# A vision tower's last LayerNorm without its mean, and uneven expert slices

## The reference

```
y       = layernorm(h)                                # no gain, eps 1e-5
logits  = y @ gate_w.T ; top 6 of 64 experts ; scores = softmax(top 6)
lattice = sum over chosen e of scores[e] * (y @ lattice_weights[e])
proj    = lattice @ out_w.T + out_b
f       = y + proj
out     = h + (f - mean(f)) * rsqrt(var(f) + 1e-5) * ln_g + ln_b
```

## Time and profile before

| | us |
|---|---|
| timed runs | 1074.19, 1078.10, 1079.18; median 1078.1 |
| profiled execution, own time | 1073.91 |
| its span, first to last instruction | 1072.0 |
| TensorE busy | 962.2 (90%) |
| VectorE busy | 617.9 (58%) |
| ScalarE busy | 397.2 (37%) |
| GpSimd busy | 151.3 (14%) |
| mean granted TensorE clock | 0.981 |

### The profile page before, as it was taken

How to read it: one execution, slowest core, us unless ns; L and a number is a source line. 1 busy time by engine, 2 the same in 40 slices (tenths; PEclk the granted TensorE clock), 3 DMA queues, 4 the chain that set the end, 5 groups by cost and what they waited for, 6 DMA issues and landing times.

```text
span 1072.0 us, 36541 instructions
## 1 busy us (share of the span) xinstructions
PE 962.2 (90%) x17004; PEld 619.3 (58%) x17004; DVE 617.9 (58%) x773; ACT 397.2 (37%) x522; POOL 151.3 (14%) x158
## 2 busy tenths in 40 slices
PE   4899999999989998999899899999888899688885
PEld 3567667667656633676567667657215677533342
DVE  2268458727844221577268458733153677779887
ACT  2442333233223486232332233233775676321100
POOL 6000000000000000000000000020010765234421
PEclk9999999999999999999999999999999899679998
DMA  6220130022021301310220230020001000000000
GB/s 197 94 79 3 60 93 24 4 94 79 4 79 61 114 6 37 109 33 4 94 79 3 67 91 18 3 94 18 14 16 42 2 2 1 2 1 1 1 11 11
DMA packets 25918, 46.78 MB, mean 44 GB/s; under 512 B 9949, under 2 KB 11000, under 8 KB 25125
## 3 DMA queue, kind: packets, MB, share of 16 engines
q1 hardware_dynamic: 24118, 42.47, 12.8%
q0 software_dynamic: 1456, 1.63, 0.6%
q10 hardware_dynamic: 192, 0.33, 0.1%
HBM read 30.25 MB, written 10.89 MB: 38 GB/s over the span
## 4 chain that ended last, share of the span: by engine, by line
PE 70%; DVE 13%; issue 6%; ACT 4%; POOL 2%; DMA 2%; SPq 1%; POOLq 0%; DVEq 0%
PE PSALL L1309 22%; PE PSALL L1277 8%; PE PSALL L1168 5%; PE PSALL L1300 5%; PE PSALL L1252 4%; PE PSALL L1182 4%; PE PSALL L536 3%; DVE WORK L1523 3%; PE PSALL L437 3%; DVE WORK L1013 2%; PE PSALL L523 2%; PE PSALL L1367 2%; DVE WORK L1542 2%; PE PSALL L1145 2%; PE PSALL L1296 2%
## 5 line engine op out<-in xcount | busy, mean ns | idle before, releaser
L1542 DVE STREAM_TRANSPOSE WORK<-PSALL 128x1024 f32<-128x1024 f32 x128 | 152.4, 1229 | 251.2 <-PE PSALL L1277 251.2
L1309 PEld LDWEIGHTS PSALL<-EW,WORK 128*64 128x64 f32 x4096 | 221.8, 138 | 72.7 <-issue 48.3
L1309 PE MATMUL PSALL<-EW,WORK 128*64 128x128 f32 x4096 | 247.6, 276 | 14.0 <-DVE WORK L1542 13.7
L1442 ACT ACTIVATE X<-PSALL,TABLES 128x1024 f32<-128x1024 f32 x128 | 141.8, 1114 | 306.5 <-PE PSALL L1309 306.5
L1523 DVE STREAM_TRANSPOSE WORK<-PSALL 128x1024 f32<-128x1024 f32 x84 | 104.3, 1241 | 32.8 <-PE PSALL L1168 31.0
L334 POOL DMA_DIRECT2D WORK<-MIXED x32 | 17.6, 550 | 665.5 <-ACT MIXED L1433 555.1
L1424 ACT COPY SPEC<-PSALL 128x400 f32<-128x400 f32 x64 | 54.4, 850 | 138.6 <-PE PSALL L1182 132.9
L1182 PEld LDWEIGHTS PSALL<-TABLES,WORK 128*64 128x64 f32 x2000 | 67.5, 139 | 47.3 <-DVE WORK L1523 31.4
L1013 DVE TENSOR_TENSOR WORK<-PSALL,X 128x832 f32<-128x832 f32 x80 | 79.3, 1017 | 16.8 <-PE PSALL L523 15.3
L1182 PE MATMUL PSALL<-TABLES,WORK 128*64 128x64 f32 x2000 | 81.1, 228 | 7.5 <-DVE WORK L1523 3.8
L1476 ACT ACTIVATE WORK<-PSALL,B 128x1024 f32<-128x1024 f32 x64 | 68.2, 1113 | 8.3 <-PE PSALL L1367 7.4
(11 more groups left out here) (157 smaller groups left out, 1153.5 us busy)
## 6 DMA issues: line engine op xcount, KB each, us to landing
SW<-in_spec_w SPq DMA_DIRECT2D x160, 80.0 KB, 2.7
spec_scr<-MIXED SPq DMA_DIRECT2D x24, 400.0 KB, 3.2
SPEC<-spec_scr SPq DMA_DIRECT2D x32, 200.0 KB
WORK<-spec_scr SPq DMA_DIRECT2D x16, 200.0 KB
WORK<-in_coords_w SPq DMA_DIRECT2D x2, 1024.0 KB, 4.8
XC<-in_coords_c SPq DMA_DIRECT2D x2, 1024.0 KB, 7.3
WORK<-MIXED SPq DMA_DIRECT2D x40, 40.0 KB
WORK<-MIXED POOLq DMA_DIRECT2D x32, 40.0 KB
```

What stands on the lines that cost most here:

```text
L1309: m = pe.matmul(PS[2 * p + z][64 * j:64 * j + 64, 2 * b * GRID:(2 * b + 2) * GRID], G[:, n % 2, b, h:h + 2, :, t].rearrange("p q o -> p (q ...
L1442: nc.scalar.activation(X[:, n].rearrange("p b (z d) c w -> p d z b (c w)", z=2)[:, p, :, :, 2 * t * GRID:2 * (t + 1) * GRID], PSALL[:, 2 * ...
L1542: nc.vector.transpose(G[:, n % 2, 2 * x + y].rearrange("p h o v -> p o h v"), PSALL[:, 4 + 2 * x:6 + 2 * x, :].rearrange("p k (h o v) -> p ...
```

## The change

The columns of out_w (laid out as 128 x 64, twice) and out_b are centred over the 64 features by the VectorE before step m = 2 of the last head; F then has a mean of zero by itself. `centre_last` is gone; GpSimd squares F directly. The slices end at images 7, 14, 21, 28 and 32. The last LayerNorm has five parts, of 8, 8, 8, 4 and 4 images; the first four lie in the loop, each with its variance and, one step later (SCALE_AT), its reciprocal and scale. Projection 6 moves from behind the loop to n = 142. For the last part the ScalarE squares (Square) while the VectorE multiplies by ln_g.

```diff
-ZT = NT // NZ
+ZI = [0, 7, 14, 21, 28, NIMG]
+ZT = 7 * TOK
-OUTPUT_AT = [84, 104, 136]
-PROJECT_AT = [n + 2 * i for n in OUTPUT_AT for i in range(LB // BC)]
+LASTS = [slice(0, 8), slice(8, 16), slice(16, 24), slice(24, 28), slice(28, NIMG)]
+PROJECT_AT = [84, 86, 104, 106, 136, 138, 142]
 ADD_AT = [n + 2 for n in PROJECT_AT]
-CENTRE_AT = [n + 6 for n in OUTPUT_AT]
-FINISH_AT = [n + 12 for n in OUTPUT_AT]
+VARIANCE_AT = [96, 116, 146, 152]
+SCALE_AT = [n + 2 for n in VARIANCE_AT]
...
@@ tail_tensor, broadcast
-                    pe.wait_ge(lo_ready, -(-(z + 1) * ZT // CT))
+                    pe.wait_ge(lo_ready, slice_chunks(z))
...
@@ tail_scalar, behind the loop over the slices
-            deviation(2, LK - 1)
+            act.wait_ge(f_ready, NC)
+            nc.scalar.activation(SQ[:, LASTS[-1]], F[:, LASTS[-1]], ACT.Square).then_inc(last_squared, 1)
+            deviation(2, len(LASTS) - 1)
...
@@ tail_pool, square; finished(k) is the gain and the residual of part k
+                    pool.wait_ge(f_ready, a.stop // BC)
+                    nc.gpsimd.tensor_tensor(SQ[:, a], F[:, a], F[:, a], ALU.mult).then_inc(squared, 1)
...
+            for k in range(len(LASTS) - 1):
                 square(2, k)
+                if k < 2:
+                    finished(k)
+            finished(2)
+            finished(3)
...
@@ tail_vector, in_head
+                if m == 2:
+                    dve.wait_ge(tail_w, 16 * TAIL_LOADS)
+                    link(nc.vector.reduce_sum(mw[:], WO[:], AX.X))
+                    link(nc.vector.reduce_sum(mo[:], OB[:], AX.X))
+                    link(nc.vector.tensor_scalar(mw[:], mw[:], 1.0 / GRID, None, ALU.mult))
+                    link(nc.vector.tensor_scalar(mo[:], mo[:], 1.0 / GRID, None, ALU.mult))
+                    nc.vector.tensor_tensor(WO[:], WO[:], mw[:].broadcast_to([128, GRID]), ALU.subtract).then_inc(ow_centred, 1)
+                    nc.vector.tensor_tensor(OB[:], OB[:], mo[:].broadcast_to([TOK, GRID]), ALU.subtract).then_inc(ob_centred, 1)
...
@@ tail_vector, in the loop
-                    if n in CENTRE_AT:
-                        centre_last(CENTRE_AT.index(n))
-                    if n in FINISH_AT:
-                        finish_last(FINISH_AT.index(n))
+                    if n in VARIANCE_AT:
+                        last_variance(VARIANCE_AT.index(n))
+                    if n in SCALE_AT:
+                        last_scale(SCALE_AT.index(n), F, ln_ready)
...
@@ tail_vector, behind the loop
-                centre_last(LK - 1)
-                finish_last(LK - 1)
-                a = slice(NIMG - LB, NIMG)
-                dve.wait_ge(ln_ready, LK)
-                link(nc.vector.tensor_tensor(TMP[:, a], TMP[:, a], rows(LNG[:], LB), ALU.mult))
+                k = len(LASTS) - 1
+                a, n = LASTS[k], NIMG - LASTS[k].start
+                dve.wait_ge(f_ready, NC)
+                nc.vector.tensor_tensor(TMP[:, a], F[:, a], rows(LNG[:], n), ALU.mult).then_inc(last_gained, 1)
+                last_variance(k)
+                dve.wait_ge(last_gained, 1)
+                last_scale(k, TMP, ln_ready)
+                dve.wait_ge(ln_ready, k + 1)
                 nc.vector.tensor_tensor(TMP[:, a], TMP[:, a], H[:, a], ALU.add).then_inc(last_ready, 1)
```

More of the change, by code:

```diff
@@ L113, in rows_step, with slice_tokens, slice_chunks @@
     return 6 + (i - ROWS_AT - 22) // 2 if i in (ROWS_AT + 22, ROWS_AT + 24) else None
+def slice_tokens(z):
+    return slice(ZI[z] * TOK, ZI[z + 1] * TOK)
+def slice_chunks(z):
+    return -(-ZI[z + 1] // BC)
 SELECTED = EXPERTS // 16
@@ L341, in tail_sync @@
             sp.dma_start(WE, w_expert).then_inc(we_in, 16)
-            for k in range(LK):
-                a = slice(k * LB, (k + 1) * LB)
-                if k < LK - 1:
+            for k, a in enumerate(LASTS):
+                if k < len(LASTS) - 1:
                     sp.wait_ge(out_ready, k + 1)
@@ L534, in expert_products @@
                     pe.wait_ge(lt_ready, z - 1)
+                w = slice_tokens(z).stop - slice_tokens(z).start
                 for i in range(2):
-                    m = pe.matmul(PS[4 + z % 2][64 * i:64 * i + GRID, 0:ZT], WE[:, ep + i, :], ZX[:, (n + i) % ZR, :],
+                    m = pe.matmul(PS[4 + z % 2][64 * i:64 * i + GRID, 0:w], WE[:, ep + i, :], ZX[:, (n + i) % ZR, 0:w],
                                   start=(ep == 0), stop=(ep == PAIRS - 2), tile_position=(0, 64 * i), skip_group_check=True)
@@ L540, in output_projection @@
             def output_projection(c):
-                pe.wait_ge(lt_ready, -(-(c + 1) * CT // ZT))
+                pe.wait_ge(lt_ready, [z for z in range(NZ) if ZI[z + 1] >= (c + 1) * BC][0] + 1)
+                pe.wait_ge(ow_centred, 1)
                 if c == 0:
@@ L578, in deviation @@
             def deviation(n, k):
-                a = slice(k * LB, (k + 1) * LB)
+                a = slice(k * LB, (k + 1) * LB) if n < 2 else LASTS[k]
                 act.wait_ge(var_ready, n * LK + k + 1)
@@ L680, in tail_scalar @@
                     deviation(2, z - 2)
+                if z == NZ - 1:
+                    deviation(2, z - 1)
                 act.wait_ge(zx_used, (z + 1) * PAIRS // 2)
-                nc.scalar.copy(LT[:, z * ZT:(z + 1) * ZT], PS[4 + z % 2][:, 0:ZT]).then_inc(lt_ready, 1)
-            deviation(2, LK - 1)
+                t = slice_tokens(z)
+                nc.scalar.copy(LT[:, t], PS[4 + z % 2][:, 0:t.stop - t.start]).then_inc(lt_ready, 1)
+            act.wait_ge(f_ready, NC)
+            nc.scalar.activation(SQ[:, LASTS[-1]], F[:, LASTS[-1]], ACT.Square).then_inc(last_squared, 1)
+            deviation(2, len(LASTS) - 1)
         def outside_sums_out(act, c):
@@ L708, in square @@
             def square(n, k):
-                a = slice(k * LB, (k + 1) * LB)
-                pool.wait_ge(centred, n * LK + k + 1)
-                nc.gpsimd.tensor_tensor(Y[:, a, 1, :] if n < 2 else SQ[:, a], TMP[:, a], TMP[:, a], ALU.mult).then_inc(squared, 1)
+                if n < 2:
+                    a = slice(k * LB, (k + 1) * LB)
+                    pool.wait_ge(centred, n * LK + k + 1)
+                    nc.gpsimd.tensor_tensor(Y[:, a, 1, :], TMP[:, a], TMP[:, a], ALU.mult).then_inc(squared, 1)
+                else:
+                    a = LASTS[k]
+                    pool.wait_ge(f_ready, a.stop // BC)
+                    nc.gpsimd.tensor_tensor(SQ[:, a], F[:, a], F[:, a], ALU.mult).then_inc(squared, 1)
             pool.wait_ge(mix_full.sem, PASSES * LAYERS * mix_full.stride)
@@ L807, in tail_pool, with finished @@
             pool.wait_ge(hl_ready, LK)
-            for k in range(LK):
-                square(2, k)
[L810 to L816, removed]
+            def finished(k):
+                a = LASTS[k]
+                n = a.stop - a.start
+                pool.wait_ge(ln_ready, k + 1)
+                nc.gpsimd.tensor_tensor(TMP[:, a], TMP[:, a], LNG[:].unsqueeze(1).broadcast_to([TOK, n, GRID]), ALU.mult
+                                        ).then_inc(scaled, 1)
+                pool.wait_ge(scaled, k + 1)
+                nc.gpsimd.tensor_tensor(TMP[:, a], TMP[:, a], H[:, a], ALU.add).then_inc(out_ready, 1)
+            for k in range(len(LASTS) - 1):
+                square(2, k)
+                if k < 2:
+                    finished(k)
+            finished(2)
+            finished(3)
         def tail_vector(dve):
@@ L997, in add_projection, with last_variance, last_scale @@
                                             F[:, a, :], ALU.add).then_inc(f_ready, 1)
[L999 to L1006, removed]
+                def last_variance(k):
+                    a = LASTS[k]
+                    if k < LK:
+                        dve.wait_ge(squared, 2 * LK + k + 1)
+                    else:
+                        dve.wait_ge(last_squared, 1)
+                    link(nc.vector.reduce_sum(st[:, 1, a], SQ[:, a], AX.X))
+                    nc.vector.tensor_scalar(st[:, 1, a], st[:, 1, a], 1.0 / GRID, EPS, ALU.mult, ALU.add).then_inc(var_ready, 1)
+                def last_scale(k, src, done):
+                    a = LASTS[k]
+                    dve.wait_ge(dev_ready, 2 * LK + k + 1)
+                    link(nc.vector.reciprocal(st[:, 3, a], st[:, 2, a]))
+                    nc.vector.tensor_tensor(TMP[:, a], src[:, a], over(st[:, 3, a], a.stop - a.start), ALU.mult).then_inc(done, 1)
                 for n in range(0, NZ * PAIRS, 2):
@@ L1012, in tail @@
                         dve.wait_ge(zx_used, (n - ZR) // 2 + 1)
-                    nc.vector.tensor_tensor(ZX[:, n % ZR:n % ZR + 2, :], PSALL[:, n % 4:n % 4 + 2, 0:ZT],
-                                            YT[:, z * ZT:(z + 1) * ZT].unsqueeze(1).broadcast_to([128, 2, ZT]), ALU.mult
+                    t = slice_tokens(z)
+                    w = t.stop - t.start
+                    nc.vector.tensor_tensor(ZX[:, n % ZR:n % ZR + 2, 0:w], PSALL[:, n % 4:n % 4 + 2, 0:w],
```

(1 more changed line is left out.)

12 lines of the change are left out of this document (9 added, 3 removed).

## The result

The changed kernel takes 1065.54 us (median of 5 runs, 1062.67 to 1069.06) against 1078.1 (1074.19 to 1079.18); the ratio is 0.9906, 95% interval 0.9884 to 0.9928. The profiled execution took 1065.44 us, its span 1063.6, against 1073.91 and 1072.0. The forecast was -9.0 us for such an execution; measured are -8.5. The ratio is the one on record; the quotient of the two medians is 0.9883, 12.6 us, and holds more of the scatter that is told of next.

What follows compares the result with a forecast made beforehand. TensorE and VectorE take turns, TensorE slightly slower per step and stalled by VectorE's LayerNorm work. Terms +3.4 - 7.4 - 4.7 - 0.3 = -9.0 us: 1069.1 us against the median 1078.1, range 1063.5 to 1074.3.

Steps and rivals of the forecast that it cites:

- the first two terms: Wider slices up to the first queued projection, +3.4 us; expert loop from there to the last product, -7.4 us.
- The wide slices: Expert loop before the first projection: 42 steps at 455 instead of 416 columns cost +3.4 us, at most 4.1.
- the sixth chunk: Slice 2 needs the sixth of eight score chunks, not the fifth; no wait counted, 1.1 us at most.
- The stalls: TensorE standing still in the later expert loop: 1.0 us per 8-image part, 2.9 in the narrow slice.
- The rule weighed: VectorE op with two SBUF inputs contends with GpSimd; scale of images 24 to 27 might lose up to 1.27 us.
- The tail: From the end of the last product to the last addition: 4.84 us instead of 9.56, so -4.7.
- The store: Last store after the last op, with half the bytes: -0.3 us, between 0 and -1.3.
- Centring the weights: Six small VectorE ops before m = 2 of the last head: cost 0, or 1.3 us without idle cover.
- (B): Narrow slice: weight loads, 1.0 us in a row, bound the 0.66 us step; -6.5 us, 1071.6 us; chance 0.07.
- (C): Tail: Square needs another table than the square root, two loads of 1.28 us; -8.2, 1069.9 us; chance 0.05.
- (D): Expert loop: TensorE's granted clock falls to half; +25 us, 1094 us, slower than before; chance 0.03.
- Rival A: Loop gains only -3.3 us, narrow slice crowded with VectorE work, wide steps cost +4.1; -4.2, 1073.9 us; chance 0.17.

## Why the prediction was right

- *The number.* 1069.1 us was given for the median, 1065.54 came. By the stretches with the end of the span the change is -9.3 against -9.0; the rest of the 12.6 us between the medians lies outside them, and the median of 1078.1 that the forecast started from was the highest of the three of the kernel before.
- *Who paces the loop* was right: TensorE's steps plus its stalls. Its account gave 45.9 us for the second stretch after, and 45.91 were measured (in the account 41.0 should be 40.9, which changes nothing); the half for before, 53.3, was 0.7 too long against 52.6, most of the difference between -7.4 and -6.7. That 45.9 was hit to the hundredth is luck: 1.0 us of it is a hold-up that the walk did not hold, and without it the stretch is 44.95. So is the sum of the first two terms: the first was 0.8 too high and the second 0.7 too low, and they cancel.
- *The wide slices*, +3.4 forecast, +2.6 measured. The step of a pair was right on both engines. The term was mis-sized because I charged every pair. Some time up to pair 41 is not set by pairs: behind each of three chains of choice the TensorE waited 0.55 us for GpSimd's scores (L702 before, L722 now), and now 0.36 to 0.37. These waits shrink, 0.5 us in all; I had not counted that. The other 0.3 us is not traced to its steps. That a broadcast would wait for the sixth chunk did not happen. The first of the three waits, before and after:

```profile
958.15 0.66 PE L487 MATMUL PSALL<-ident,X 65*96 65x65 f32 x8 [0.55 <-POOL X L702]
...
959.61 0.66 PE L499 MATMUL PSALL<-ident,X 65*96 65x65 f32 x8 [0.37 <-POOL X L722]
```

- *The stalls*: 1.0 forecast for each wide part, 0.5 and 0.8 measured; 2.9 forecast for the narrow slice, some 3.4 measured (the 3.1 above, and 0.3 at the last products). But these 3.4 hold one thing that I had put in the wrong place: the hold-up by GpSimd, 1.0 us. Without it the narrow slice would have stalled by 2.4.
- *The rule weighed* came true in another instruction. I had looked for it at the scale with its two inputs in SBUF, and gave it 1.27 us at most; it came at the small scaling three VectorE instructions before, for 0.97. It was left out of the sum, with no chance of its own.
- *The tail*: 4.84 forecast, 4.86 measured, each term within 0.1. The copy's 0.37 was a near neighbour for Square (0.42). The recorded bounds of -5.0 and -4.1 are not quite what the two rows for Square give, -4.8 and -4.1; the measured -4.7 lies inside both. *The store*: -0.3 forecast, -0.5 measured.
- *Centring the weights* costs nothing: the six ops end at 768.62 in the VectorE's order of time and the next op of the head starts at 769.10, 2.37 us after the one before it, as ever, with 0.48 idle left of the 1.62 of the earlier trace rows:

```profile
767.40 0.21 DVE L895 TENSOR_REDUCE mw<-WO 128x1 f32<-128x64 f32 x1
...
768.41 0.21 DVE L900 TENSOR_TENSOR OB<-OB,mo 65x64 f32<-65x64 f32 x1
769.10 0.75 DVE L1642 TENSOR_SCALAR WORK<-PSALL,B 128x512 f32<-128x512 f32 x1 [0.48 <-PE PSALL L1455]
```

- The rivals: the weight loads (B) did not show, the narrow step was 0.65; no table load (C); the granted clock, 0.50 to 0.54 from 940 to 950 us in both kernels, was 1.00 from 950 us to the end of the last product (D). Rival A, that the narrow slice gives the gain back, was wrong for the sum, but what it said of the crowded slice is what the run with a last part of 8 found: 1.9 us of it.
- What the forecast did not see is whose gain it was. It summed the change's effects and never each part's alone. The LayerNorm alone brings 9.1 of 9.3 us; slices, the moved projection and the part of 4 add 0.2 together, since +2.6 in the first stretch and the hold-up pay for what they gain at the end.

## What to carry to other kernels

A matmul whose result is only centred afterwards can be centred in its weights: three vector ops a part became six small ones in the whole kernel, and since the removed ops stood in the loop's stalls, the loop gained more than their own time (6.3 us, for 4.6 us of VectorE work and 0.8 of its waits for the root). How much of that surplus comes from setting variance and scale one product apart is not shown. Cutting the last piece smaller trades the tail against a busier loop in front of it: price both, and each part of a change by itself. And when a second engine is given work at the same time, look at the duration of the small VectorE ops beside it, not only at waits: in the trace of the kernel before, one such row was already three times as long as its like.

## What the runs showed of the hardware

- A VectorE tensor_scalar on 65 x 4 fp32 values with both operands in SBUF took 1.14 us beside a GpSimd tensor_tensor that had started 0.15 us earlier, and ended with it; with its input in PSUM it took 0.16 us beside the same op. No wait is shown for it. In the kernel before, one on 65 x 8 took 0.51 instead of 0.17.
- Beside the same GpSimd ops a reciprocal on 65 x 4 (0.17 us) and a reduction of 65 x 256 (0.41 us), both SBUF to SBUF, were not held up; a tensor_tensor with two SBUF inputs was, by 0.29 us for an overlap of 0.43 and by 0.07 for 0.20. In the five meetings read here the second op was longer by the overlap less 0.13 to 0.14 us.
- Matmuls of 260 columns, fp32 and bf16 in turn on two halves of the array, kept to what their columns ask (steps of eight instructions: 0.65 us at 260 columns, 1.05 at 416, 1.15 at 455), weight loads of 111 and 139 ns hidden.
- A square root with its bias from SBUF and a scale took 0.30 us on 65 x 4 values, without them 0.20.
